# Fp4 network of a fused two-layer block: two-tensor scale steps, another order of VectorE's turn, split transposes, and a last turn on VectorE alone

## The reference

```python
def fp4_quant_dequant(x):                      # along the last dim, blocks of 16
    xb = x.reshape(shape[:-1] + (shape[-1] // 16, 16))
    scale = jnp.maximum(jnp.max(jnp.abs(xb), axis=-1, keepdims=True) / 6.0, 1e-12)
    xn = xb / scale
    idx = jnp.searchsorted(_MID, jnp.abs(xn))
    return (_GRID[idx] * jnp.sign(xn) * scale).reshape(shape)

def fp4_linear(x, w):                          # x and w both quantised
    return jnp.einsum('bsk,nk->bsn', fp4_quant_dequant(x), fp4_quant_dequant(w))

gate = fp4_linear(x, w_gate)                   # 128 -> 352
y = fp4_linear(x, w_up)                        # 128 -> 352
out = fp4_linear(jax.nn.silu(gate) * y, w_down)   # 352 -> 128
# x = x + gb * out, with gb one factor per feature and batch
```

## Time and profile before

| | |
|---|---|
| time, median of 3 runs | 1154.24 us (1153.39 to 1157.0) |
| time of the profiled execution | 1158.26 us |
| its span, first to last instruction | 1156.4 us |
| busy share of the span: PE, DVE, ACT, POOL | 77%, 69%, 38%, 12% |
| the fp4 network in the span | from 972.87 us to the end |

### The profile page before, as it was taken

How to read it: one execution, slowest core, us unless ns; L and a number is a source line. 1 busy time by engine, 2 the same in 40 slices (tenths; PEclk the granted TensorE clock), 3 DMA queues, 4 the chain that set the end, 5 groups by cost and what they waited for, 6 DMA issues and landing times. The chain is left out here.

```text
span 1156.4 us, 20054 instructions
## 1 busy us (share of the span) xinstructions
PE 891.3 (77%) x7220; PEld 502.5 (43%) x7220; DVE 795.2 (69%) x1440; ACT 439.1 (38%) x786; POOL 139.5 (12%) x108
## 2 busy tenths in 40 slices
PE   5429999999898866999735747999996984576774
PEld 4116766666565532433212313443434842343442
DVE  0762344788878885999978835878873333899982
ACT  3524666656545423554314540110112255222221
POOL 3520000000000001000004760000000000123231
PEclk8857999999989877999977888999998796787786
DMA  7400000000000001554341346665640000000000
GB/s 187 68 1 2 2 3 3 3 3 3 2 2 2 2 1 64 198 196 173 144 128 73 119 145 219 199 203 189 208 146 0 1 1 1 1 0 18 9 19 27
DMA packets 53988, 79.80 MB, mean 69 GB/s; under 512 B 14288, under 2 KB 28432, under 8 KB 53776
## 3 DMA queue, kind: packets, MB, share of 16 engines
q1 hardware_dynamic: 49680, 76.57, 20.9%
q10 hardware_dynamic: 4224, 2.10, 0.6%
HBM read 40.90 MB, written 35.65 MB: 66 GB/s over the span
## 5 line engine op out<-in xcount | busy, mean ns | idle before, releaser
L1466 PE MATMUL bank<-ex_hh,Wd 128*128 128x512 f32 x256 | 130.2, 601 | 7.3 <-DVE ex_hh L1527 7.3
L1163 ACT ACTIVATE so_u<-bank,bu 128x512 f32<-128x512 f32 x128 | 87.8, 686 | 113.0 <-PE bank L57 112.9
L1527 DVE TENSOR_TENSOR ex_hh<-ex_pg,bank 128x512 f32<-128x512 f32 x128 | 84.3, 673 | 46.4 <-DMA ex_pg<-hidden 26.9
L882 ACT ACTIVATE att_qk<-bank 128x512 f32<-128x512 f32 x128 | 66.8, 601 | 46.1 <-PE bank L712 45.6
L970 DVE TENSOR_TENSOR att_am<-bank,causal 128x512 f32<-128x512 f32 x64 | 44.0, 687 | 51.3 <-PE bank L746 51.2
L746 PE MATMUL bank<-att_qk 64*128 64x128 f32 x1024 | 78.2, 295 | 0.0
L1148 POOL TENSOR_TENSOR so_made<-so_u,so_g 128x512 f32<-128x512 f32 x33 | 54.7, 1672 | 193.9 <-ACT so_g L1169 188.2
L746 PEld LDWEIGHTS bank<-att_qk 64*128 64x128 f32 x1024 | 65.6, 196 | 20.8 <-issue 20.8
L1267 DVE SCALAR_TENSOR_TENSOR so_made<-bank,bg,so_u 128x512 f32<-128x512 f32 x95 | 68.9, 744 | 8.2 <-DMA hidden<-so_made 4.0
L1466 PEld LDWEIGHTS bank<-ex_hh,Wd 128*128 128x128 f32 x256 | 47.8, 192 | 57.6 <-issue 32.7
L55 PE MATMUL bank<-Hhi,Wgh 128*128 128x512 f16 x128 | 51.3, 401 | 27.0 <-DVE so_made L1267 14.8
(11 more groups left out here) (379 smaller groups left out, 1852.9 us busy)
## 6 DMA issues: line engine op xcount, KB each, us to landing
hidden<-so_made SPq DMA_DIRECT2D x128, 256.0 KB, 2.0
ex_pg<-hidden SPq DMA_DIRECT2D x64, 512.0 KB, 3.8
xin<-in_L_attn_x_dram ACTq DMA_DIRECT2D x8, 256.0 KB, 7.6
out_dram<-ff_ot SPq DMA_DIRECT2D x8, 256.0 KB, 2.3
so_other<-so_key SPq DMA_DIRECT2D x2, 512.0 KB, 5.5
wm<-in_L_wmod_dram SPq DMA_DIRECT2D x2, 384.0 KB, 5.8
F<-so_fhi SPq DMA_DIRECT2D x2, 256.0 KB, 4.0
F<-so_flo SPq DMA_DIRECT2D x2, 256.0 KB, 4.1
```

Source lines behind the costliest of these rows:

```text
L882: nc.scalar.activation(qk[t % 2][:, r, :, :].rearrange("p a l -> p (a l)"), psF[r], ACT.Relu).then_inc(s_["fe"], 1)
L1163: nc.scalar.activation(u[m % 4][:], psU[q][:, :], ACT.Silu, bias=bu[:, k:k + 1], scale=1.0 / WS).then_inc(s_u[q], 1)
L1466: nc.tensor.matmul(psY[j][:, :], Wd[:, n, :], hh[n % 4][:], start=False, stop=n == EBLK - 1).then_inc(s_dn[n % 4], 1)
L1527: nc.vector.tensor_tensor(hh[k % 4][:], pg[k // 2 % 4][:, k % 2, :], psW[k % 4][:, :], ALU.mult).then_inc(s_hh[k % 4], 1)
```

## The change

`fp4_rounding` and `fp4_quant` are cut into three parts (normalise, grid, scale). The scale step and the multiplication by the reciprocal become `scalar_tensor_tensor`; the separate step that lowers the reciprocal goes away, because the factor is taken into the multiplication. A constant tile `tiny` of 128 x 88 holds 1e-12.

DVE's turn becomes: `quantise_hidden(t)`, `gated(t+1, 0)`, `gated(t+1, 1)`, `normalise_x(t+2)`, `gated(t+1, 2)`, `add_x(t-1)`, `gated(t+1, 3)`, `quantise_x(t+2)` (grid and scale only). PE's `by_token(t+3)` now waits only for the normalisation and moves between the two gate-and-up pairs; `out_by_token(t-1)` and the three groups of `hidden_back` are spread between the other groups. ACT's list follows. In the last turn DVE itself does what GpSimd does in the others, and the three groups of transposes go to three banks.

```diff
-    step(nc.vector.tensor_scalar(sc, sc, 1.0 / 6.0, 1e-12, ALU.mult, ALU.max))
+    step(nc.vector.scalar_tensor_tensor(sc, sc, 1.0 / 6.0, w["tiny"][:, 0:n // 16], ALU.mult, ALU.max))
     step(nc.vector.reciprocal(rc, sc))
-    step(nc.vector.tensor_scalar(rc, rc, 1.0 - 2.0 ** -24, None, ALU.mult))
-    step(nc.vector.tensor_tensor(blocks(xn), blocks(src), by_block(rc), ALU.mult))
+    return nc.vector.scalar_tensor_tensor(blocks(xn), blocks(src), 1.0 - 2.0 ** -24, by_block(rc), ALU.mult, ALU.mult)
+def fp4_grid(nc, step, n, w):
+    xn, m = w["xn"][:, 0:n], w["m"][:, 0:n]
     step(nc.vector.tensor_scalar(m.bitcast(U32), xn.bitcast(U32), 0x7F800000, None, ALU.bitwise_and))
     step(nc.vector.tensor_scalar(m, m, 1.0, 1.5 * 2.0 ** 22, ALU.max, ALU.mult))
     return nc.vector.tensor_tensor(xn, xn, m, ALU.add)
+def fp4_scale(nc, step, dst, n, w):
     step(nc.vector.tensor_tensor(xn, xn, w["m"][:, 0:n], ALU.subtract))
     return nc.vector.tensor_tensor(blocks(dst), blocks(xn), by_block(w["sc"][:, 0:n // 16]), ALU.mult)
...
@@ constants, GpSimd @@
+                    step(nc.gpsimd.memset(tiny[:], 1e-12))
...
@@ PE @@
                         def by_token(t):
-                            upto(pe, s_xq, t)
+                            upto(pe, s_xn, t)
                         def quantised_back(t):
-                            upto(pe, s_e4, t - 3)
+                            upto(pe, s_e4, t - 2)
...
                         def turn(t, follow, behind):
                             if follow > 0:
                                 gate_up(t + 1, 2)
+                            if follow > 2:
+                                by_token(t + 3)
+                            if follow > 0:
                                 gate_up(t + 1, 3)
+                            if behind:
+                                out_by_token(t - 1)
+                            hidden_back(t, 0, psT)
                             if follow > 1:
                                 quantised_back(t + 2)
-                            if follow > 2:
-                                by_token(t + 3)
-                            hidden_back(t)
+                            hidden_back(t, 1, psT if follow > 0 else psH)
                             if follow > 1:
                                 gate_up(t + 2, 0)
+                            hidden_back(t, 2, psT if follow > 0 else psU[0])
+                            if follow > 1:
                                 gate_up(t + 2, 1)
                             down(t)
-                            if behind:
-                                out_by_token(t - 1)
...
@@ ACT: take_h(t+3) first, then both silus, take_out(t-1), take_hidden(t, 0), take_x(t+2), take_hidden(t, 1), silu(t+2, 0), take_hidden(t, 2), silu(t+2, 1) @@
...
@@ DVE @@
+                        def normalise_x(t):
+                            upto(dve, s_T1, t + 1)
+                            fp4_normalise(nc, step, psH[:, :], ST, work_x).then_inc(s_xn, 1)
                         def quantise_x(t):
+                            upto(dve, s_xn, t + 1)
+                            step(fp4_grid(nc, step, ST, work_x))
                             upto(dve, s_T2, t)
-                            fp4_quant(nc, step, psH[:, :], xq[:], ST, work_x).then_inc(s_xq, 1)
+                            fp4_scale(nc, step, xq[:], ST, work_x).then_inc(s_xq, 1)
...
+                        def scale_hidden(t):
+                            upto(dve, s_round, t + 1)
+                            upto(dve, s_T3, t * 3)
+                            fp4_scale(nc, step, hq[:], CH * I_FF, work_h).then_inc(s_hq, 1)
...
                         def turn(t, ahead1, ahead2, behind):
                             quantise_hidden(t)
+                            if not ahead1:
+                                scale_hidden(t)
                             if ahead1:
                                 gated(t + 1, 0)
                                 gated(t + 1, 1)
                             if ahead2:
-                                quantise_x(t + 2)
+                                normalise_x(t + 2)
+                            if ahead1:
+                                gated(t + 1, 2)
                             if behind:
                                 add_x(t - 1)
                             if ahead1:
-                                gated(t + 1, 2)
                                 gated(t + 1, 3)
+                            if ahead2:
+                                quantise_x(t + 2)
...
@@ GpSimd @@
-                        with pool.Fori(0, NT) as t:
+                        with pool.Fori(0, NT - 1) as t:
```

More of the change, by code:

```diff
@@ L148, in program @@
         eps_ln = sb("eps_ln", [P, 1])
+        tiny = sb("tiny", [P, ST // P * I_FF // 16])
         mod = sb("mod", [P, 2, 6, NB])
@@ L283, in program @@
             work |= {k: tb("prep_" + k, [P, QW // 16]) for k in ("sc", "rc")}
+            work["tiny"] = tiny
             xin = tb("xin", [P, 8, 4, P])
@@ L1738, in fp4_network @@
                 work_h |= {k: tb(k + "_h", [P, CH * I_FF // 16]) for k in ("sc", "rc")}
+                work_x["tiny"] = work_h["tiny"] = tiny
                 psH, psX, psT, psY = bank[0], bank[1], bank[6], bank[7]
@@ L1743, in fp4_network @@
                                              "T4", "e4", "out", "dve"))
-                s_round, s_grid = sem("ff_round"), sem("ff_grid")
+                s_xn, s_hn, s_round, s_grid = (sem("ff_" + n) for n in ("xn", "hn", "round", "grid"))
                 def upto(eng, s, n):
@@ L1783, in gate_up, with hidden_back @@
                             nc.tensor.matmul(psU[c % 2][:, 0:I_FF], x_c, wuT[:], start=True, stop=True).then_inc(s_GU, 1)
-                        def hidden_back(t):
+                        def hidden_back(t, k, ps):
+                            n = NBLK[k]
                             upto(pe, s_hq, t + 1)
-                            for k, n in enumerate(NBLK):
+                            if ps is psT:
                                 upto(pe, s_e3, t * 3 + k)
-                                for c in range(CH):
-                                    at = c * I_FF + k * P
-                                    m = nc.tensor.transpose(psT[0:n, c * P:(c + 1) * P], hq[:, at:at + n], ident[:])
-                                m.then_inc(s_T3, 1)
+                            for c in range(CH):
+                                at = c * I_FF + k * P
+                                m = nc.tensor.transpose(ps[0:n, c * P:(c + 1) * P], hq[:, at:at + n], ident[:])
+                            m.then_inc(s_T3, 1)
                         def down(t):
@@ L1853, in silu, with take_hidden @@
                             nc.scalar.activation(sg[c % 2][:], psG[c % 2][:, 0:I_FF], ACT.Silu).then_inc(s_sg, 1)
-                        def take_hidden(t):
+                        def take_hidden(t, k, ps):
+                            n = NBLK[k]
                             upto(act, s_Y, t)
-                            for k, n in enumerate(NBLK):
-                                upto(act, s_T3, t * 3 + k + 1)
-                                nc.scalar.copy(hqT[0:n, k, :], psT[0:n, :]).then_inc(s_e3, 1)
+                            upto(act, s_T3, t * 3 + k + 1)
+                            nc.scalar.copy(hqT[0:n, k, :], ps[0:n, :]).then_inc(s_e3, 1)
                         def take_out(t):
@@ L1880, in turn @@
                                 silu(t + 1, 3)
-                            if follow > 2:
-                                take_h(t + 3)
+                            if behind:
+                                take_out(t - 1)
+                            take_hidden(t, 0, psT)
                             if follow > 1:
                                 take_x(t + 2)
-                            take_hidden(t)
+                            take_hidden(t, 1, psT if follow > 0 else psH)
                             if follow > 1:
                                 silu(t + 2, 0)
+                            take_hidden(t, 2, psT if follow > 0 else psU[0])
+                            if follow > 1:
                                 silu(t + 2, 1)
-                            if behind:
-                                take_out(t - 1)
                         turns(act, prologue, turn)
@@ L1912, in quantise_hidden @@
                             upto(dve, s_hq, t)
[L1913 removed]
+                            fp4_normalise(nc, step, hh[:], CH * I_FF, work_h).then_inc(s_hn, 1)
+                            upto(dve, s_hn, t + 1)
+                            fp4_grid(nc, step, CH * I_FF, work_h).then_inc(s_round, 1)
+                        def scale_hidden(t):
+                            upto(dve, s_round, t + 1)
+                            upto(dve, s_T3, t * 3)
+                            fp4_scale(nc, step, hq[:], CH * I_FF, work_h).then_inc(s_hq, 1)
                         def add_x(t):
@@ L1922, in prologue @@
                         def prologue():
```

(9 more changed lines are left out.)

22 lines of the change are left out of this document (13 added, 9 removed).

## The result

| | before | changed |
|---|---|---|
| median, same session | 1153.82 us (1152.62 to 1157.0, 4 runs) | 1142.59 us (1139.78 to 1143.73, 4 runs) |
| profiled execution, span | 1158.26, 1156.4 us | 1139.78, 1138.0 us |
| granted clock over the span | 0.877 | 0.887 |
| fp4 network | 972.87 to 1156.4: 183.5 us | 970.71 to 1138.0: 167.3 us |

What follows compares the result with a forecast made beforehand. DVE was taken to set the turn (busy 18.94 of 19.80 us), with small steps held by GpSimd's passes. Terms -1.3 +0.6 -3.45 -2.3 -1.6 -6.3 = -14.35 us gave 1139.9 from 1154.24, range 1129 to 1148.

Steps and rivals of the forecast that it cites:

- The scale step is held: DVE's x row: scale step held by GpSimd's first pass, normalising free, ending R+4.40 (R: end of wide row's last rounding step).
- rivals A and D: A: scale step free, turn 17.1, total 1130, chance 12%; D: normalising held to second pass's end, turn 20.9, 1151.5, 4%.
- The new wait: Before DVE's last product: gate_up(t+1, 3) stands behind by_token(t+3) on PE; DVE waits about 1.1 or 2.7 us.
- The clock in the middle turns: PE at 2.4 or 1.2 GHz in turns 1 to 4: 18.5 or 20.15; three in four fast, 18.9, -3.45 us.
- T = G + 3.25 + 7.8: Middle turn R to R: G, when x's grid starts after R, plus 3.25 to the wide row, plus its 7.8 us.
- Turn 0: First turn, before without add_x: the same PE chain sets it, 18.5 to 20.15 us, taken 19.6, +0.6.
- Rival B: Middle turns gain nothing, PE being at 1.2 GHz whenever by_token comes: turn 20.15, total 1147, chance 15%.
- Turn 5: Turn without by_token: gate_up 3 follows 2 directly, turn 17.45, -2.3 us.
- Prologue: Before the first R: DVE's 2.23 us idleness goes, PE's chain starts some 1.1 earlier; -1.3 us (bounds -0.2, -2.8).
- Turn 6: Turn without x tile, bounded by when PE is free: 12.1 to 14.4 us, taken 13.05, -1.6.
- The tail: Last wide row to end: down starts at R+8.3, -3.2; DMA wait shorter, -2.0; taken -6.3 (bounds -5.2 and -8.4).
- rival C: PE becomes the bound, staying at 1.2 GHz through down: turn 22.6, total +13, 1167, slower; chance 4%.

Runs made afterwards that it cites:

- e1: The changed kernel with the small scale step a tensor_scalar again, its old form: 1143.21 us, ratio 0.9908 to the kernel before.
- e2: The changed kernel with PE's by_token(t+3) moved behind gate_up(t+1, 3): 1134.82 us, ratio 0.9834 to the kernel before.
- e4: The changed kernel with the last wide row's two steps given back to GpSimd: 1147.72 us, ratio 0.9942 to the kernel before.
- e11: The changed kernel with the last turn's three groups of transposes through one bank, interleaving kept: 1146.92 us, ratio 0.9936 to the kernel before.
- e6: e2 with DVE's wait on its own last x step moved from the loop's end to the next normalisation: 1126.43 us, ratio 0.9752 to the kernel before.
- e7: e2 with an own scale tile for the last wide row, its wait for GpSimd moved behind the reduction: 1131.54 us, ratio 0.9786.
- e10: e9 plus e5b's edit, no small scale step in x rows: 1129.81 us, ratio 0.9786 to the kernel before.
- e8: The changed kernel with the wide row's transposes in one block behind quantised_back and through one bank: 1155.47 us, ratio 1.0001 to the kernel before.
- e3: The kernel before with only the reciprocal's small step fused into the normalising multiplication: 1151.70 us, ratio 0.9975.
- e5b: The changed kernel without the small scale step in x rows, by_token still early: 1132.06 us, ratio 0.9808 to the kernel before.
- e9: The changed kernel with the edits of e2, e6 and e7 together: 1126.25 us, ratio 0.9763 to the kernel before.

## Why the prediction was right, and where it was not

- **The scale step is held; the normalising step is not.** Both right: 1.79 and 0.69 us, normalising ends at R+4.40 as worked out, and e1 shows that the form does not matter. This step decided between the forecast and rivals A and D.
- **The new wait.** Right in place and size: the product ends at R+7.43 (forecast 7.45), DVE idles 1.42 (forecast 1.1), because its own list is 0.4 us shorter than worked out (in e2 the grid starts at R+5.84, forecast R+6.35). e2 removes the wait and nothing else, and T falls to what DVE's list allows.
- **The clock in the middle turns.** I gave three in four to 2.4 GHz; in the profiled execution all four were fast, in those of e4 and e11, whose turns are the same code, three of four (turn 4 20.29, DVE waiting 2.89 where I had worked out 2.7). So the same turn can take 1.5 us more in one execution than in another. In the fast ones the term was 18.5, measured 18.82. The missing 0.3 is not the clock but the 0.51 us at the loop's edge: from the grid to the wide row are 3.66 us, not the 3.25 of T = G + 3.25 + 7.8, since in the kernel before the x row was followed by add_x in the middle of the turn, with a gap of 0.19; e6 shows it. That 18.9 was taken and 18.82 measured is luck: the share of slow turns that I counted in did not come, and the edge that I had not seen made up for it.
- **Turn 0** was the slow case, 20.15, the upper bound to 0.01. Rival B's mechanism is real, but it came in single turns, not in all.
- **Turn 5** 17.10 for 17.45. **Prologue** -1.46 for -1.3; DVE's second tile starts without the idle time of the earlier trace rows.
- **Turn 6** 13.91 for 13.05: it gave half of the 1.6 forecast. I bounded it by PE alone, and the lower bound of 12.1 left out that the last wide row overwrites a tile that GpSimd is still reading (its scales). It waits until R+6.1. e7 shows it: 1.4 us.
- **The tail** -8.76 for -6.3, beyond the fast bound of -8.4. The mechanism was right, the clock mis-sized: I took the transposes as slow and down as slow for the most part, and all of it ran at 2.4 GHz. Down starts 4.55 earlier (3.2 forecast) and is 2.1 shorter, and the DMA wait is worth the 2.0 forecast. e4 and e11 each lose 5.6 us there, and in both the transposes and down run at 1.2 GHz. So in these executions neither edit alone kept the clock. Both together don't ensure it: e10 has both, and its down took 5.34.
- **The step that failed, without touching the number:** "hidden_back interleaved saves PE's idle 0.7 us between groups, beside DVE's 7.8 us of wide row: nothing." The term came out unharmed, since I priced the kernel as it is, but the reason was wrong. Undone, it takes back 8.6 of the gain, and with the three banks all of it (e11, e8). I had rival C's price ready (PE late beyond R+4 at the low clock) and named the slack as 2 us, and did not see that the interleaving is what keeps PE from it. In the old order the block did no harm: in e3 gate_up(t+1, 2) starts at R+3.6 and DVE waits 0.83 us for a product, but that comes out of the held scale step (0.87 long instead of 1.79), and T is 18.62.
- **The total.** The terms sum to -16.2 in the profiled pair, -14.35 was forecast, the medians say -11.2. 1142.59 lies in the forecast's range, and the gain is 3.1 us less than forecast. The terms hold for one profiled execution each: that of the kernel before stood 4.4 above its median, and that of the changed kernel was the fastest of four. Where the 2.2 us ahead of the stage come from is open. One reading was miscounted, without effect on the sum: from 1019.06 to 1117.88 there are six starts of the first pass, with five spaces of 19.76.

Of what the change joins, fusing the factor brings 1.2 us a turn, the last turn's two edits 5.1 and 4.3 (each taken away alone), the interleaving 8.6 in the new order (taken away behind the banks; these three don't add up to the gain), the scale step's form nothing, and by_token's new place costs 1.5 a turn.

## What to carry to other kernels

When a step is moved ahead in one engine's list because its input is ready sooner, look at what is queued behind it: an early wait on PE delayed the product that DVE needed, and moving it down one place was worth 7.8 us. A step held by another engine's pass is not shortened by rewriting it; the hold goes to the next step of the same kind, until the pass itself is the bound. Round trips between transposes and copies should be filled with other matmuls when the engine's list has little slack: in e8 their idle time was less than a quarter of the 3.6 us that the list grew by, and about half was the lower clock of what ran with and behind them.

## What the runs showed of the hardware

- The same 32-element step took 0.19 us between two GpSimd passes, 1.79 under the first and 2.51 when it started 0.12 us behind the second. Held were tensor_scalar (one tensor in SBUF; e1, and the grid's first step in e3, e5b and e10) and scalar_tensor_tensor with both tensors in SBUF. Not held were the reciprocal (0.35) and steps with one input in a bank (0.69 for 512 elements, 0.52 for the products).
- A wait of DVE on its own last step, at the edge of its loop, cost 0.7 us a turn (e6); in the middle of a turn it left 0.19.
- The idle time just ahead did not tell PE's clock: in a middle turn by_token took 0.66 behind 1.87 us in the changed kernel and 0.96 behind 1.91 in e11, followed by gate_ups at 0.76 and 1.38; e8's wide transposes, with 0.7 us gaps, were followed by gate_ups of 1.38. In the tail the same six matmuls took 2.84 or 2.85 us in the changed kernel, e1, e2, e5b, e6, e7 and e9, and 4.98 to 5.41 in the kernel before, e3, e4, e8, e10 and e11.
